# First attention of a two-layer decoder: one block of value products a turn, and the keys' projection ahead of the transposes

## The reference, cut to what matters

```python
h = layernorm(x)
q = einsum('bsf,hfd->bhsd', h, wq)      # 16 heads of 64; k and v likewise
attn = softmax(q @ k.T / sqrt(64))      # 512 x 512 for each batch and head
out = einsum('bhst,bhtd->bhsd', attn, v)
x = x + out.transpose(0, 2, 1, 3).reshape(4, 512, 1024) @ wo
```

## Time and profile before

| | us |
|---|---|
| median of 3 runs | 1529.1 (1527.95 to 1529.73) |
| the profiled execution: time / span | 1523.41 / 1521.2 |
| TensorE busy in the span | 1315.4 (86%) |
| VectorE, ScalarE, GpSimd busy | 1058.3, 714.1, 551.5 |
| start of turn 0's scores | 13.9 |
| end of the first attention | about 485 |

### The profile page before, as it was taken

How to read it: one execution, slowest core, us unless ns; L and a number is a source line. 1 busy time by engine, 2 the same in 40 slices (tenths; PEclk the granted TensorE clock), 3 DMA queues, 4 the chain that set the end, 5 groups by cost and what they waited for, 6 DMA issues and landing times.

```text
span 1521.2 us, 29546 instructions
## 1 busy us (share of the span) xinstructions
PE 1315.4 (86%) x10964; PEld 953.1 (63%) x10964; DVE 1058.3 (70%) x2533; ACT 714.1 (47%) x1462; POOL 551.5 (36%) x556
## 2 busy tenths in 40 slices
PE   8999999999997798334699887789889788879998
PEld 5667677677675465222376455566666666758887
DVE  5998777777776787781033458888979987866554
ACT  4666666666665464100023154456555555524222
POOL 3555565565553000106112275632433342211110
PEclk9999999999998899557799989999999898999999
DMA  5130000000002000000022214211311211000000
GB/s 183 29 126 15 1 2 1 2 1 1 2 1 63 1 2 1 1 0 15 23 76 73 43 38 116 64 32 28 65 30 33 59 30 28 22 1 1 1 0 28
DMA packets 76999, 47.01 MB, mean 31 GB/s; under 512 B 26090, under 2 KB 68667, under 8 KB 76871
## 3 DMA queue, kind: packets, MB, share of 16 engines
q1 hardware_dynamic: 72342, 41.71, 10.5%
q10 hardware_dynamic: 2480, 2.29, 0.5%
q0 software_dynamic: 2048, 1.27, 0.4%
HBM read 21.89 MB, written 10.49 MB: 21 GB/s over the span
## 4 chain that ended last, share of the span: by engine, by line
PE 64%; DVE 25%; ACT 5%; issue 3%; another core or an unknown queue 2%; ACTq 0%; DMA 0%; POOL 0%; DVEq 0%
PE psum L1138 7%; PE psum L1123 7%; PE psum L1526 6%; PE psum L1639 6%; PE psum L1113 6%; DVE negmax L2240 4%; PE psum L1538 4%; PE psum L1650 4%; PE psum L1510 2%; PE psum L1349 2%; PE psum L1517 2%; PE psum L1089 2%; PE psum L1318 2%; PE psum L1147 2%
## 5 line engine op out<-in xcount | busy, mean ns | idle before, releaser
L582 POOL TENSOR_TENSOR arena<-arena,rden 128x512 f32<-128x512 f32 x256 | 260.9, 1042 | 209.7 <-DVE rden L1785 209.6
L786 ACT ACTIVATE arena<-psum,negmax 128x512 f32<-128x512 f32 x256 | 175.1, 693 | 150.9 <-DVE negmax L1776 131.6
L1776 DVE TENSOR_REDUCE negmax<-psum 128x1 f32<-128x512 f32 x256 | 168.1, 682 | 55.5 <-PE psum L1113 54.9
L2240 DVE TENSOR_REDUCE negmax<-psum 128x1 f32<-128x512 f32 x256 | 164.8, 685 | 51.6 <-PE psum L1517 44.9
L1123 PEld LDWEIGHTS psum<-cst,arena 128*128 128x128 f32 x1024 | 113.1, 140 | 44.7 <-issue 44.3
L1123 PE MATMUL psum<-cst,arena 128*128 128x128 f32 x1024 | 138.1, 276 | 3.2 <-DVE arena L1771 0.8
L650 POOL TENSOR_TENSOR a_qblk<-a_qstack,cst 96x512 fp32r<-96x512 f32 x64 | 68.5, 1071 | 125.7 <-PE psum L1517 116.3
L1113 PE MATMUL psum<-a_qk 64*128 64x512 f32 x768 | 105.9, 407 | 2.5 <-DVE a_qk L1794 2.5
L1510 PE MATMUL psum<-a_kstack,a_qblk 96*128 96x512 f32 x256 | 101.6, 480 | 5.7 <-POOL wqkv L653 5.7
L975 ACT ACTIVATE kT<-psum,negmax 128x512 f32<-128x512 f32 x64 | 44.0, 688 | 131.5 <-DVE negmax L2240 81.2
L1639 PE MATMUL psum<-f_h,f_w 128*128 128x512 f32 x384 | 100.3, 411 | 2.5 <-DVE arena L2370 2.5
(11 more groups left out here) (324 smaller groups left out, 2847.5 us busy)
## 6 DMA issues: line engine op xcount, KB each, us to landing
a_kstack<-a_khi SPq DMA_DIRECT2D x128, 64.0 KB
w<-in_ew SPq DMA_DIRECT2D x2, 2048.0 KB, 8.4
a_kstack<-a_klo SPq DMA_DIRECT2D x64, 64.0 KB
xs_rows<-f SPq DMA_DIRECT2D x3, 1024.0 KB, 5.3
arena<-xs_rows SPq DMA_DIRECT2D x8, 384.0 KB, 3.7
ys_rows<-wqkv SPq DMA_DIRECT2D x8, 384.0 KB, 2.6
a_qstack<-a_qhi SPq DMA_DIRECT2D x120, 16.0 KB, 1.8
X<-in_x SPq DMA_DIRECT2D x4, 256.0 KB, 9.6
```

Of the source, the lines that this page charges most:

```text
L582: pool.tensor_tensor(a0_p[u % 4], a0_p[u % 4], rden[:, u:u + 1].broadcast_to([P, SEQ]), ALU.mult).then_inc(a0_norm, 1)
L786: act.activation(a0_p[u % 4], bank[u % 4][:, :], ACT.Exp, bias=negmax[:, u:u + 1], accum_out=den[:, u:u + 1]).then_inc(a0_exp, 1)
L1776: dve.tensor_reduce(negmax[:, u:u + 1], bank[u % 4][:, :], AX.X, ALU.max, negate=True).then_inc(a0_max, 1)
L2240: dve.tensor_reduce(negmax[:, n % 8:n % 8 + 1], bank[n % 4][:, :], AX.X, ALU.max, negate=True).then_inc(a1_max, 1)
```

## The change

The second half of a turn's value products no longer stands at the end of the second half of the next turn but directly behind the first half of them, at the end of the next turn's first half. The keys' projection of the next turn goes ahead of the transposes of units 0 and 1. On ScalarE the copy of unit 1 goes behind the copy of the keys. On VectorE the copy of unit 0 goes behind the low part of the keys, and this is one maximum earlier than it was.

```diff
@@ -807,10 +807,10 @@
 
             def a0_second_half(g):
                 a0_exp_of(g, 4)
-                a0_copy(g, 1)
                 a0_exp_of(g, 5)
                 if g < PAIRS - 1:
                     a0_copy_k(g + 1)
+                a0_copy(g, 1)
                 a0_exp_of(g, 6)
                 a0_exp_of(g, 7)
                 a0_copy(g, 3)
@@ -1123,21 +1123,21 @@
                     mm = pe.transpose(bank[4 + u % 2][:, kt * P:(kt + 1) * P], a0_p[u % 4][:, kt * P:(kt + 1) * P], ident)
                 mm.then_inc(a0_t, 1)
 
-            def a0_values(g, half):
-                for copied in (a0_tcd, a0_tca):
-                    pe.wait_ge(copied, g * UH + half * 2 + 2)
-                if half == 0:
-                    pe.wait_ge(a0_vc, g + 1)
-                    if g:
-                        pe.wait_ge(a0_x, g)
-                    else:
-                        pe.wait_ge(pre_act, 1)
-                qs = slice(half * 2 * P, (half + 1) * 2 * P)
-                for kt in range(QT):
-                    for h in range(2):
-                        mm = pe.matmul(bank[7][h * DK:(h + 1) * DK, qs], a0_vtok[g % 2][:, kt, h * DK:(h + 1) * DK],
-                                       a0_pT[g % 2][h][:, kt, qs], start=(kt == 0), stop=(kt == QT - 1))
-                mm.then_inc(a0_pv, 1)
+            def a0_values(g):
+                pe.wait_ge(a0_vc, g + 1)
+                if g:
+                    pe.wait_ge(a0_x, g)
+                else:
+                    pe.wait_ge(pre_act, 1)
+                for half in range(2):
+                    for copied in (a0_tcd, a0_tca):
+                        pe.wait_ge(copied, g * UH + half * 2 + 2)
+                    qs = slice(half * 2 * P, (half + 1) * 2 * P)
+                    for kt in range(QT):
+                        for h in range(2):
+                            mm = pe.matmul(bank[7][h * DK:(h + 1) * DK, qs], a0_vtok[g % 2][:, kt, h * DK:(h + 1) * DK],
+                                           a0_pT[g % 2][h][:, kt, qs], start=(kt == 0), stop=(kt == QT - 1))
+                    mm.then_inc(a0_pv, 1)
 
             def a0_output(g):
                 pe.wait_ge(a0_ftc, g + 1)
@@ -1168,7 +1168,7 @@
                 if g < PAIRS - 1:
                     a0_project_q(g + 1)
                 if g:
-                    a0_values(g - 1, 0)
+                    a0_values(g - 1)
 
             def a0_second_half(g):
                 a0_scores(g, 2)
@@ -1176,14 +1176,12 @@
                 if g == 0:
                     context_values(7, x0w[:, 4, :], x0rows[:, 0, :])
                     pe.wait_ge(pre_dve, 3)
+                if g < PAIRS - 1:
+                    a0_project_k(g + 1)
                 a0_turn_t(g, 0)
                 a0_turn_t(g, 1)
-                if g < PAIRS - 1:
-                    a0_project_k(g + 1)
                 a0_turn_t(g, 2)
                 a0_turn_t(g, 3)
-                if g:
-                    a0_values(g - 1, 1)
 
             pe.wait_ge(ld_w0, 48)
             a0_project_q(0)
@@ -1196,8 +1194,7 @@
             a0_output(PAIRS - 2)
             a0_turn_t(PAIRS - 1, 6)
             a0_turn_t(PAIRS - 1, 7)
-            a0_values(PAIRS - 1, 0)
-            a0_values(PAIRS - 1, 1)
+            a0_values(PAIRS - 1)
             a0_output(PAIRS - 1)
 
 
@@ -1818,13 +1815,13 @@
             def a0_second_half(g):
                 a0_maximum(g, 4)
                 a0_maximum(g, 5)
-                a0_copy(g, 0)
                 a0_maximum(g, 6)
                 a0_reciprocal(g, 4)
+                if g < PAIRS - 1:
+                    a0_low_k(g + 1)
+                a0_copy(g, 0)
                 a0_maximum(g, 7)
                 a0_reciprocal(g, 5)
-                if g < PAIRS - 1:
-                    a0_low_k(g + 1)
                 a0_copy(g, 2)
                 a0_reciprocal(g, 6)
                 a0_reciprocal(g, 7)
```

## The result

| | before | changed |
|---|---|---|
| median (4 runs each), us | 1528.53 (1519.16 to 1529.73) | 1685.07 (1673.31 to 1685.82) |
| ratio | | 1.103, 95% interval 1.100 to 1.107 |
| profiled execution: time / span | 1523.41 / 1521.2 | 1685.57 / 1683.4 |
| first attention, from turn 0's scores to its last matmul | 13.9 to 483.3 | 13.9 to 640.8 |
| all behind it | 1037.9 | 1042.6 |

157.5 us of the profiled difference of 162.2 lie in the first attention. The 4.7 behind it are in code that is the same; on other chips and in other runs that part took between 1004 and 1044 us, so they are not put down to the change.

A forecast was written before the change was run, and what follows sets the result against it. TensorE was taken to bound the kernel, with no idle time in a steady turn. To 1529.1 us it added 118 for waits (114 over 31 turns, 4 in early turns) and 37 for the clock: 1684 us, range 1636 to 1712.

The forecast's parts named there:

- The walk of the second half: Steady turn's chain through ScalarE and VectorE: unit 2's transposes at 6.64, next scores at 7.61, turn 17.91 instead of 14.23 us.
- The second scores: Next turn's second scores wait for ScalarE to read unit 7's banks: start at 8.98 instead of 8.40, a 0.58 us wait.
- The moved value records: The second 16 value records, now behind the first 16, add 1.72 us to the first half.
- the price of an entry: One entry into the value products on TensorE, saved by the merged block: 0.1 to 0.15 us.
- The early turns and the end: Early turns, with layer norm steps delaying maxima, cost 4 us more; the last turn, without keys' projection, costs 0.
- The clock: TensorE's pause of 3.1 us brings a half-clock stretch in nearly each turn: 1.2 us each, 31 x 1.2 = 37.
- The bounds of 0.6 and 1.7: Price per turn of one 3.41 us half-clock stretch on TensorE: at least 0.6 us, at most 1.7 us.
- 114 + 4 + 37 = 155: Added time: 114 us for waits in 31 turns, 4 for early turns, 37 for the clock.
- 1 (the clock stays up): Rival: the waits come in the first attention but TensorE's clock stays up, 1647 us; chance 20%.
- 2 (the clock does not recover in one stretch): Rival: TensorE's clock stays low longer or drops twice a turn, 1.7 to 3 us a turn, 1718 us; chance 13%.
- 3 (faster by the saved switch): Rival: waits don't bind and TensorE's saved tiling-mode switch shows, 1529 - 5 = 1524 us; chance 3%.
- 4 (only the bank is waited for): Rival: unit 2's transposes wait only for the bank, next scores at 5.1, turn 14.9, 1548 us; chance 3%.

The follow-up runs named there:

- the filled kernel: Changed kernel plus ten unread products of 128 columns in TensorE's pause of each second half; ratio 1.079 to the kernel before, in both runs.
- Keys only: Kernel before with the keys' projection and the two copies moved as in the change, values left in two parts; ratio 1.112.
- Copies back: Changed kernel with the copies of units 0 and 1 at their old places on VectorE and ScalarE; ratio 1.050 to the kernel before.
- late, tuned: Kernel before with one value block ending the second half, unit 0's copy ahead of unit 5's maximum, layer norm steps in second halves; ratio 0.995.
- block only: Kernel before with the 32 value records in one block behind the first half, keys and copies as before; ratio 1.025.
- the two fillings: Unread products in TensorE's waits: ten in the changed kernel (ratio 1.079), four in the one with copies at old places (1.045, from 1.050).

## Why the prediction was right

**The walk of the second half** held to 0.03 us up to the next scores (table above). The second scores came at 8.87 and not at 8.98, 0.11 early, and the step behind them took 0.11 more than the 0.79 priced; the two cancel, so that the transposes behind them start at 454.39 - 444.62 = 9.77 as forecast. The moved value records cost 3.60 - 1.88 = 1.72 us from start to start, as the walk had it. Two readings in it were loose and changed nothing: the price of an entry set a busy time of 3.67 against distances of 1.88, where distances throughout give 2 x 1.88 - 3.60 = 0.16; and today's transposes of unit 2 start at 302.26 in the timeline, the chain's 302.42 is where they become what is waited for. The turn at full clock, 17.91 predicted, is shown by the filled kernel: 20 steady turns of it took 357.4 us (229.67 to 587.12) against 283.7: 3.69 a turn, predicted 3.68.

**The early turns and the end.** These are read from the filled kernel's second profile, which has no low stretch, and from the kernel before on the same chip. The time from turn 0's scores to the start of the steady turns is 214.9 (13.81 to 228.76) against 171.1: 43.9 more, predicted 11 x 3.68 + 4 = 44.5, so the early turns cost 3.4 beyond the walk where I took 4. The last turn's second half and the stage's end, for which I had put nothing, take 14.8 us in the changed kernel against 14.6. So the waits cost 43.9 + 73.8 + 0.2 = 117.9 us, predicted 118.

**The clock.** 38.5 us in the stage, predicted 31 x 1.2 = 37. The changed kernel had 31 low stretches in the first profile, one a turn, and 30 in the second, where one turn with the same pause had none and took 19.06 us, the filled kernel's 19.04. I had it as one stretch of 3.4 us in nearly each turn with a few that don't recover; in fact 20 were 3.4 and 11 (10 in the second profile) were 6.8 us long. In the steady stretch a cycle of three turns repeats, with 19.03, 20.21 and 18.79 us, that is 1.1, 2.3 and 0.9 for the clock. The bounds of 0.6 and 1.7 for a single stretch hold there; the double one is what I had as a rival's price of 1.7 to 3. So single stretches cost a little less than I took and every third steady turn was the rival's case. The mean was 1.4 in the steady turns and 0.9 in the early ones (28.9 us in 20 and 9.6 in 11, changed against filled on one chip); that it came out at 1.2 is partly luck. Keys only shows the same reasoning off by a factor of two, because it asked neither how often the stretch is a double one nor how much of it falls on TensorE's own work. Copies back shows that my view of which pauses matter was too narrow.

**The sum.** 114 + 4 + 37 = 155 stands against 157.5 in the stage and 156.5 between the medians. The agreement to 1 us in the whole is luck: the part behind the attention alone varies by several us from run to run.

**The rivals.** 1 (the clock stays up) is what the filled kernel shows: 119.9 us over the kernel before on its chip, forecast 118. 2 (the clock does not recover in one stretch) came true for 11 turns of 31. 3 (faster by the saved switch) fails at this place, but its price was right: 0.15 us a turn, shown where no wait takes its place, in late, tuned. 4 (only the bank is waited for) is near copies back, whose real turn is 16.2 and not 14.9, because I left out of it the wait for the low part of the keys: the next scores start at 6.45 (414.93 to 421.38) and not at 5.1.

The rule of the Trainium skill (TensorEngine Tiling, Key Properties) that a change of tiling mode drains the engine fits that 0.15 us, the one switch a turn fewer; no run separates the switch from the rest of the step. What it says of transposes (TensorE: Matmul & The Clock Gate, Part 4), that they don't count as busy time for the clock the way other work does, is not tested by these runs: the two fillings are plain products, with as many transposes beside them as before.

## What to carry to other kernels

Before merging two blocks of the engine that sets the pace, ask what the half that they leave has to cover: the chain from its first result through the other engines to its next need has a length of its own (here 5.54 us in block only, 6.45 in copies back), and work taken from above it turns into a wait. Walk that chain with starts from the trace, each engine's queue in its order; a copy that is queued behind another product's copy inherits all of that one's waits. Price a pause twice: for itself and for the half clock behind it, and look at how much of the engine's own work the slow stretch meets.

## What the runs showed of the hardware

The clock fell though no single pause was over 1.16 us: 8 times in copies back, with pauses of 0.44 and 1.16 in one turn, and not once in these turns when the second was filled, nor in block only with one pause of 1.12. A pause of 3.06 us with work around it brought a low stretch in 31 and 30 of 31 turns of the changed kernel, and 26 stretches in keys only. A low stretch of 3.4 us cost nothing at one place (copies back, 48.7 us), about 1 us in the changed kernel and 1.6 in keys only. Ten products whose results nobody reads made the changed kernel 42 us faster. In keys only each late turn is 20.48 us long, with a slow stretch of 6.8 us at the same place of it.
